# Order of statistics, keys and shared weights around the attention loop of a gated cross-attention and expert layer

## The reference

```
x = x + tanh(g_xattn) * LN'( attention( LN(x), context ) )       # 16 heads of 64, one learned null key and value
h = LN(x)
x = x + tanh(g_ffn) * ( shared_expert(h) + sum over the 8 best of 32 experts of weight * expert(h) )
expert(h) = ( silu(h Wg + bg) * (h Wu + bu) ) Wd + bd            # 256 -> 128 -> 256
weight = sigmoid(logit) / sum of the 8 sigmoids
```

## Time and profile before

| | us |
|---|---|
| median of 3 runs | 2310.6 |
| lowest, highest | 2310.09, 2318.49 |
| the profiled execution | 2310.3 |
| its span | 2308.6 |

### The profile page before, as it was taken

How to read it: one execution, slowest core, us unless ns; L and a number is a source line. 1 busy time by engine, 2 the same in 40 slices (tenths; PEclk the granted TensorE clock), 3 DMA queues, 4 the chain that set the end, 5 groups by cost and what they waited for, 6 DMA issues and landing times. The chain is left out here.

```text
span 2308.6 us, 44550 instructions
## 1 busy us (share of the span) xinstructions
PE 2080.1 (90%) x14386; PEld 1908.5 (83%) x14386; DVE 1837.3 (80%) x4287; ACT 1532.5 (66%) x4478; POOL 1299.8 (56%) x1444
## 2 busy tenths in 40 slices
PE   8999679999999999999998599999999999999992
PEld 7888578888889899888888478988888888888881
DVE  5444357888888888888888566877999999999994
ACT  5433346676767777766766235888888887888881
POOL 1000213777777777777777540001777777777776
PEclk9999889999999999999999799999999999999996
DMA  9987489987878878787887699989999999999995
GB/s 318 322 284 263 137 281 311 323 267 256 264 263 267 265 246 264 261 266 257 267 264 243 204 389 357 298 296 303 398 405 405 402 397 393 390 398 394 395 394 170
DMA packets 385092, 708.51 MB, mean 307 GB/s; under 512 B 136380, under 2 KB 248989, under 8 KB 382397
## 3 DMA queue, kind: packets, MB, share of 16 engines
q1 hardware_dynamic: 335708, 562.99, 70.1%
q0 software_dynamic: 49152, 142.67, 16.9%
HBM read 348.18 MB, written 357.30 MB: 306 GB/s over the span
## 5 line engine op out<-in xcount | busy, mean ns | idle before, releaser
L1472 POOL DMA_INDIRECT parts<-results_dram,kept_index x512 | 531.6, 1038 | 411.2 <-DMA results_dram<-y 246.0
L776 POOL DMA_INDIRECT pages_dram<-rows,kept_index x472 | 473.2, 1003 | 138.1 <-issue 120.0
L845 ACT ACTIVATE exps<-sim,minus_max 128x78 f32<-128x78 f32 x1024 | 319.1, 355 | 37.9 <-DVE minus_max L923 35.1
L1503 ACT ACTIVATE y<-yps,row_weight 128x256 f32<-128x256 f32 x636 | 246.9, 470 | 1.2 <-PE yps L134 1.2
L845 ACT ACTIVATION_READ_ACCUMULATOR exps<-sim,minus_max 128x1 f32 x1024 | 240.3, 235 | 0.0
L1494 ACT ACTIVATE w_h<-w_raw 128x768 fp32r<-128x768 f32 x159 | 137.3, 863 | 85.4 <-DMA w_raw<-in_experts 85.3
L1681 PE MATMUL xps<-ident,xin 128*128 128x128 f32 x1272 | 168.6, 276 | 28.1 <-DVE wq_l L1543 16.0
L132 PE MATMUL yps<-w_h,hid_h 128*128 128x256 f32 x636 | 179.4, 282 | 2.1 <-ACT y L1503 2.1
L133 PE MATMUL yps<-w_h,hid_l 128*128 128x256 f32 x636 | 179.8, 283 | 0.0
L134 PE MATMUL yps<-w_l,hid_h 128*128 128x256 f32 x636 | 179.2, 282 | 0.0
L1524 ACT ACTIVATE hid_h<-hidden 128x512 fp32r<-128x512 f32 x175 | 110.2, 630 | 101.4 <-DVE hidden L1634 96.9
(11 more groups left out here) (270 smaller groups left out, 7530.8 us busy)
## 6 DMA issues: line engine op xcount, KB each, us to landing
xin<-pages_dram SPq DMA_DIRECT2D x159, 576.0 KB, 9.6
results_dram<-y SPq DMA_DIRECT2D x159, 512.0 KB, 8.8
pages_dram<-blank SPq DMA_DIRECT2D x108, 576.0 KB, 3.6
w_raw<-in_experts SPq DMA_DIRECT2D x159, 385.0 KB, 9.3
pages_dram<-blank SPq DMA_DIRECT2D x12, 1728.0 KB, 7.0
keys_h_dram<-keys_h SPq DMA_DIRECT2D x32, 624.0 KB, 5.8
keys_l_dram<-keys_l SPq DMA_DIRECT2D x32, 624.0 KB, 7.6
kT_h<-keys_h_dram SPq DMA_DIRECT2D x32, 624.0 KB, 5.6
```

What stands on the lines that cost most here:

```text
L776: pool.indirect_dma_start(dram["pages"], bass.IndirectOffsetOnAxis(ap=kept_index[:, at:at + 1].bitcast(U32), axis=0), buffer(batch)[:, k / ...
L845: last = act.activation(exps[u % 2][:, h, :], scores(u)[:, h // 4, h % 4, :], ACT.Exp, bias=minus_max[u][:, h:h + 1], accum_out=row_sum[u] ...
L1472: pool.indirect_dma_start(parts[slot(batch, t)][:, k, :], None, done, bass.IndirectOffsetOnAxis(ap=kept_index[:, at:at + 1].bitcast(U32), ...
L1503: last = act.activation(y[s][:, q, :], yps[:, q, :], ACT.Copy, scale=row_weight[s][:, q:q + 1])
```

## The change

Five edits, all in the order of the lists:

- **Statistics.** VectorE works kind 0 right behind kind 2 at T3b instead of at Q3. GpSimd makes its rstd right behind that of kind 2, ahead of scatter 12. ScalarE applies kind 2 behind PV1a's high half instead of ahead of it.
- **First scores.** Units 0 and 1 wait for the low half of Q1 and no longer of Q3; they use heads of Q0 and Q1 only. Units 2 and 3 still wait for Q3.
- **Keys and null rows.** In iteration 0 SyncE waits for the scores and loads batch 1's keys ahead of the first fill and of the values. The null rows of the second value buffer are placed behind batch 1's values in iteration 0, with a semaphore of their own; those of the first stay in iteration -1.
- **Shared weights.** VectorE and ScalarE scale and split them in iteration 32 behind N2, not in iteration 33 ahead of it.
- **Last store of weights.** The semaphores of the routing weights live across the two stages; the wait for the last batch's goes from the attention stage's end to load 4 of the expert stage.

```diff
@@ attention_phase, SyncE
+            def place_nulls(i):
+                rest = v_rest[i][:, :, :, :, :].rearrange("p s f q d -> p (s f) q d")
+                for head in range(PAIRS):
+                    sp.dma_start(rest[(head + 1) * REST - 1:(head + 1) * REST, :, head // 2, head % 2 * DH:(head % 2 + 1) * DH].bitcast(F32),
+                                 null_rows[:, :, :, :].rearrange("p s f d -> p (s f) d").bitcast(F32)).then_inc(null_placed[i], 16)
...
+                if b == 0:
+                    sp.wait_ge(sim_full, UNITS)
+                    load_keys(1)
                 fill_pages(b, 0)
...
-                    for v in v_rest:
-                        rest = v[:, :, :, :, :].rearrange("p s f q d -> p (s f) q d")
-                        for head in range(PAIRS):
...
+                    place_nulls(0)
+                if b == 0:
+                    place_nulls(1)
                 fill_pages(b, 1)
-                if 0 <= b <= B - 2:
+                if 1 <= b <= B - 2:
                     sp.wait_ge(sim_full, UNITS * (b + 1))
                     load_keys(b + 1)
...
             for i in range(BUFFERS):
-                sp.wait_ge(weights_stored[i], 16 * len(range(i, B, BUFFERS)))
+                if i != (B - 1) % BUFFERS:
+                    sp.wait_ge(weights_stored[i], 16 * len(range(i, B, BUFFERS)))
@@ GpSimd
                 if 1 <= b <= B:
                     make_rstd(2, b - 1)
+                if b <= B - 3:
+                    make_rstd(0, b + 2)
                 if scatters:
                     scatter(b, range(12, 13))
...
-                if b <= B - 3:
-                    make_rstd(0, b + 2)
@@ ScalarE
-                if b == B + 1:
-                    act.wait_ge(shared_gated, 1)
...
+                    if name == "N2" and b == B:
+                        act.wait_ge(shared_gated, 1)
+                        act.activation(ahead["shared_split"][0][:, :], shared[:, :], ACT.Copy).then_inc(shared_hi, 1)
...
-                    if name == "Q3" and 1 <= b <= B:
+                    if name == "PV1a" and 1 <= b <= B:
...
                         apply(2, buffer(b - 1)[:, :, 0:D], lambda t: x1[1 - par][:, t, :], b - 1)
@@ VectorE
-                if b == B + 1:
-                    dve.wait_ge(ahead_loaded, 144)
...
+                    if name == "N2" and b == B:
+                        dve.wait_ge(ahead_loaded, 144)
...
                     if name == "T3b" and 1 <= b <= B:
                         dve.wait_ge(summed, b)
                         statistics(2, lambda t: x1[1 - par][:, t, :], b - 1)
+                    if name == "T3b" and b <= B - 3:
+                        dve.wait_ge(x_loaded, 16 * (b + 2))
+                        statistics(0, lambda t: x_in[:, t, :], b + 2)
...
-                    if name == "Q3" and b <= B - 3:
-                        dve.wait_ge(x_loaded, 16 * (b + 2))
-                        statistics(0, lambda t: x_in[:, t, :], b + 2)
@@ TensorE
-                pe.wait_ge(ring_lo, nth(EVICTED, "Q3", b - 1))
+                pe.wait_ge(ring_lo, nth(EVICTED, "Q3" if u // 2 else "Q1", b - 1))
...
-                    if b == 0:
-                        pe.wait_ge(null_placed, 32 * PAIRS)
+                    if b <= 1:
+                        pe.wait_ge(null_placed[b], 16 * PAIRS)
@@ expert_phase, SyncE
             def load_weights(n):
                 if n >= DEPTH:
                     sp.wait_ge(x_full, DC * (n - DEPTH + 1))
+                if n == DEPTH:
+                    last = (B - 1) % BUFFERS
+                    sp.wait_ge(weights_stored[last], 16 * len(range(last, B, BUFFERS)))
```

More of the change, by code:

```diff
@@ L459, in weight_views, with attention_phase @@
             w[:, 2 * DC * I:EW])
-def attention_phase(nc, ctx, dram, wq, wo, opened_by, rows, kept_index, ahead):
+def attention_phase(nc, ctx, dram, wq, wo, opened_by, rows, kept_index, ahead, weights_stored):
     def sb(name, shape, dt=F32):
@@ L554, in attention_phase @@
     x1_stored = [sem(f"x1_stored{i}") for i in range(2)]
-    weights_stored, scattered = ([sem(f"{n}{i}") for i in range(BUFFERS)] for n in ("weights_stored", "scattered"))
+    scattered = [sem(f"scattered{i}") for i in range(BUFFERS)]
     x2_stored = sem("x2_stored")
@@ L1059, in step @@
                     prepare()
-                if b == B + 1:
-                    dve.wait_ge(ahead_loaded, 144)
[L1062 to L1068, removed]
-                    dve.tensor_tensor(ahead["bias_stack"][low_rows, :], bias_rows[low_rows, :],
-                                      ahead["bias_stack"][low_rows, :].bitcast(F32), ALU.subtract)
-                    dve.tensor_tensor(shared_row_split[1][:, :], shared_row[:, :], shared_row_split[0][:, :].bitcast(F32),
-                                      ALU.subtract).then_inc(shared_row_ready, 1)
                 if here:
@@ L1081, in step @@
                     low(name, b)
+                    if name == "N2" and b == B:
+                        dve.wait_ge(ahead_loaded, 144)
+                        down = shared[:, 2 * DC * I:EW]
+                        dve.tensor_scalar(shared_row[:, :], shared_row[:, :], gate2[0:1, 1:2], None, ALU.mult)
+                        dve.tensor_scalar(down, down, gate2[:, 1:2], None, ALU.mult).then_inc(shared_gated, 1)
+                        dve.wait_ge(shared_hi, 3)
+                        dve.tensor_tensor(ahead["shared_split"][1][:, :], shared[:, :],
+                                          ahead["shared_split"][0][:, :].bitcast(F32), ALU.subtract)
+                        low_rows = slice(2 * ROUTED, 3 * ROUTED)
+                        dve.tensor_tensor(ahead["bias_stack"][low_rows, :], bias_rows[low_rows, :],
+                                          ahead["bias_stack"][low_rows, :].bitcast(F32), ALU.subtract)
+                        dve.tensor_tensor(shared_row_split[1][:, :], shared_row[:, :], shared_row_split[0][:, :].bitcast(F32),
+                                          ALU.subtract).then_inc(shared_row_ready, 1)
                     if name == "T3b" and 1 <= b <= B:
@@ L1233, in xT_ahead, with expert_phase @@
     return [[w[:, :, i * PAGE:(i + 1) * PAGE] for w in wq] for i in range(INNER // PAGE)]
-def expert_phase(nc, ctx, dram, opened_by, rows, kept_index, ahead, wq):
+def expert_phase(nc, ctx, dram, opened_by, rows, kept_index, ahead, wq, weights_stored):
     def sb(name, shape, dt=F32):
@@ L1749, in sb @@
             return across.enter_context(nc.sbuf_tensor(name, shape, dt))
+        weights_stored = [across.enter_context(nc.semaphore(f"weights_stored{i}")) for i in range(BUFFERS)]
         opened_by = sb("opened_by", [P, B * ROUTED])
```

15 lines of the change are left out of this document (6 added, 9 removed).

## The result

| | before | after |
|---|---|---|
| median, us | 2314.6 (4 runs) | 2351.4 (4 runs) |
| profiled execution, us (its span) | 2310.3 (2308.6) | 2356.1 (2354.4) |

The changed kernel takes 1.0165 times as long [1.0145, 1.0184]: 37 us more by the medians, 46 between the two profiled executions. The direction was forecast, the size wasn't: 14 us were forecast, and 2351.4 lies outside the range of 2294 to 2334.

The account below looks back on a forecast made before the run. The loop was taken as bound by first maximum, exponentials, unit 3's scores, TensorE to Q0 and VectorE's backlog. 2310.3 + 19.5 (loop) - 3 (opening) - 2.6 (end) gave 2324 us; range 2294 to 2334.

Parts of the forecast that it names:

- What sets the period: Regular iteration, 30.07 us: first maximum, two units of exponentials, unit 3's scores, TensorE to Q0, VectorE's backlog, next maximum.
- the wait for X: TensorE's transposes of normalised tokens waited 34.7 us in the loop; removing this was to gain 0.0 an iteration, bounds 0 to 1.3.
- The collision: GpSimd's earlier product z times scale holds VectorE's L937 and L938 of unit 3: +1.08 an iteration, +29.2 us.
- Rival (a): VectorE's L937 goes ahead of GpSimd's product; period and half-clock time stay: 2305 us, chance 0.24.
- (b): VectorE goes first and the half-clock stretches vanish with the wait for X: 2286 us, chance 0.10.
- (c): The opening keeps its 8.90 us as gain and VectorE goes first: 2299 us, chance 0.08.
- 8.90: TensorE's wait in us for batch 1's keys, issued behind its values; forecast to go when the keys are issued first.
- Half clock: Loop iterations with TensorE's clock at 0.50: six as before, 1.52 each, 9.1 us in place of 18.8.
- T3a's wait: TensorE's transposes T3a wait for the outputs' low half; forecast to grow by 1.08 us in a regular iteration.
- rival (d): As forecast, but half the loop's iterations hold a half-clock stretch, eight more: 2336 us, chance 0.08.
- The opening: Up to batch 4: keys 1's wait goes, keys 2's becomes some 11 us; -3 us, bounds +1 and -9.
- The end: Last iterations: weight split moves into VectorE's idle (1.6 us), SP's store wait leaves (0.98); -2.6 us, bounds 0 and -4.

Follow-up runs that it names:

- after_product_later: Changed kernel with one more GpSimd scatter ahead of the product z times scale and one fewer behind its sum; 2312.8 us, 1.0005 of before.
- before_product_earlier: Kernel before with one GpSimd scatter moved from ahead of the product z times scale to behind it; 2331.4 us, 1.0082 of before.

## Why the prediction was wrong in size

**What sets the period: right.** X no longer waits in the loop, and the scores of unit 3 start at 1005.98, 0.15 behind unit 1's last row sum. The idle moved as said, 1.18 in two pieces (0.26 and 0.92) where 1.1 was forecast ahead of unit 3's alone. That the wait for X wasn't worth its 34.7 us was shown by the pair of kernels with the product later: 0.08 of regular period an iteration.

**The collision: right by its mechanism, with luck in the margin.** GpSimd came 0.55 earlier against the first maximum, just what was asked (0.55) and less than the 0.64 to 0.77 that I had found; the scatter in front took 1.40 instead of 1.04 and ate the rest. So the head start of 0.05 was there only in the 12 iterations with a stretch behind the scores' idle. In the 15 others the product is recorded 0.01 behind L945, and L945 is held all the same: that the tie went this way no row had shown. L945 takes 1.79 to 1.88 in every iteration, the period is 31.24 (forecast 31.15), and 26 x 31.24 + 30.13 for the last one is 842.4: +30.5 against +29.2. In the kernel before, the product moved by one scatter gave the same 31.18. Rival (a) fell: L937 won in no iteration of the changed kernel, and with it fell (b) and (c), of which (c) also had the whole 8.90 kept as a gain at batch 4. By the rule of the Trainium skill ("SBUF — State Buffer", "Who interferes with whom") whichever of the two issues first holds the port; the three positions of the product agree (L937 of unit 3 at 1.79 with the product 0.05 ahead, 0.69 with L938 at 1.37 when it is 0.54 behind, 0.69 and 0.27 when it comes after both). For the tie of 0.01 the recorded starts can't tell who issued first.

**Half clock: the step that failed.** I took six stretches "as before, since the idle time that remains is as long", at 1.52 each: 9.1. There are 26, 12 behind the scores' idle and 14 behind T3a's wait. What is over the regular periods is 872.7 - 842.4 = 30.3, against 18.8 before: +11.5 instead of -9.7, and this 21.2 is two thirds of the 31.9 us by which the two profiled executions differ from the forecast's +13.9. The price was right where I had it: an iteration with a stretch behind the scores' idle alone takes 32.78, 1.54 more. Its count was wrong, 12 for six, some 9 us. What I left out is a second kind, 14 at about 0.9 each (32.15), some 12 us, 21 to 23 us behind the first maximum and just behind T3a's wait. The prediction had that wait growing by 1.08 and gave it no stretch. Its upper bound, one iteration in three, was a guess, too low; rival (d) had the direction, and its 2336 the same fault. Whether each place of idle alone does it was then measured: T3a's 1.34 with X's 1.27 makes 6, the scores' 1.19 alone 9 (after_product_later), and only with T3a's 1.34 and the scores' 1.19 together are there 24 and 26. In the loops of these kernels all stretches but one begin just behind one of these waits. Why this pair is hit so much more often than the pair in before_product_earlier isn't settled. The length of the wait alone doesn't decide it: in the kernel before X waits 1.3 in all 27 iterations, and six of the seven stretches come in every fourth iteration, 122.88 us apart. The Trainium skill ("TensorE: Matmul & The Clock Gate", "HAM oscillation — how this bites in real kernels") has gaps let the clock fall, in its example waits for a DMA of some 3 to 5 us; the trace agrees that it falls behind gaps, in the kernels before and after with waits of 0.92 to 1.44 us just in front, but the sum of TensorE's three longest waits in the loop, 62.5 us before and 76.9 after, doesn't give 7 and 26.

**The opening: wrong mechanism.** Forecast -3, measured +4.1 (+3.0 alone). The steps around it:

```profile
282.91 0.34 SPq L611 DMA_DIRECT2D kT_h<-keys_h_dram  x1
...
284.24 6.21 SPq L621 DMA_DIRECT2D v_main<-values_dram  x2
...
300.66 4.95 SPq L665 DMA_DIRECT2D v_rest<-null_rows  x8
...
335.38 1.00 SPq L611 DMA_DIRECT2D kT_l<-keys_l_dram  x1
...
345.23 0.47 PE L132 MATMUL sim<-kT_h,qT_h 128*128 128x156 f32 x1 [15.73 <-issue]
...
389.31 1.64 POOL L784 DMA_INDIRECT pages_dram<-rows,kept_index  x1 [8.60 <-DMA pages_dram<-blank]
```

The 8.90 did go, as forecast. Keys 2 were to be issued about 331.5 and come in at 342; they were issued at 335.38 and the scores waited 15.73 instead of 11. SP stands still until 282.9 for unit 3's scores, v_main behind the keys takes 6.21 instead of 3.42, and with the second null rows the fill behind stands at 305.7 and not 302.3. But by the runs above the mis-sized SP queue isn't what set batch 4: it follows GpSimd's first scatter, which waits for the fills. The kernel before shows GpSimd waiting 9.42 for them at 386.81, and I read TensorE's waits there, not GpSimd's.

**The end: right steps, wrong bound.** The profile of after:

```profile
1324.10 0.76 DVE L952 BATCH_NORM_STATS2 stats<-ring 128x6 f32<-128x256 f32 x2 [1.44 <-PE ring L134]
...
1337.47 0.69 DVE L1058 TENSOR_TENSOR x2T_l<-ring,x2T_h 128x512 fp32r<-128x512 f32 x1 [2.30 <-ACT x2T_h L865]
...
1346.94 0.17 DVE L1050 TENSOR_SCALAR kept_index<-top_key 128x16 int32<-128x16 f32 x1
...
1352.24 0.20 POOL L1464 MEMSET ident<- 128x128 f32 x1 [7.51 <-POOLq L606]
```

Measured from the low half of N2 that precedes the split (1271.72 in the kernel before, 1318.12 here: 46.40 on), VectorE's statistics come at the same time (1277.70, 1324.10), so the split is covered; the last low half of N2 comes 1.48 sooner (forecast 1.6), and so does the routing's last row. But the expert stage starts only 0.59 sooner. In the kernel before:

```profile
1302.01 0.17 DVE L1042 TENSOR_SCALAR kept_index<-top_key 128x16 int32<-128x16 f32 x1
...
1306.43 0.20 POOL L1451 MEMSET ident<- 128x128 f32 x1 [7.51 <-POOLq L606]
```

In both kernels, and in every other kernel of the study, it starts 7.51 behind the end of GpSimd's last scatter, while VectorE's idle at this place is 4.35 in one and 5.23 in the other. SyncE's waits ended at 1303.7 in the kernel before, 2.7 ahead of the stage. GpSimd's queue bounded this end; the store's landing (0.98) was hidden, so taking SP's wait away was worth nothing. -2.6 should have been -0.6.

**The sum.** With the half clock as measured it would have been +13.9 + 21.2 = +35, and with the opening and the end +44; the profiled executions differ by 45.8.

## What to carry to other kernels

Ask of a wait of the busiest engine whether another wait stands behind it: this one was 34.7 us long and worth 0.08 of regular period an iteration, until VectorE's backlog was cut; then the same edit was worth 0.66. When an edit makes a queue earlier, list what its instructions will meet: GpSimd 0.55 us earlier cost 1.17 an iteration, and one scatter moved, or 0.65 us of VectorE's backlog moved, turned the same change from 1.0165 to 1.0005 and 0.9870 of before. At the opening and at a stage's end read the waits of every queue for the one that ends last, GpSimd's too, before any other is given a price.

## What was not expected of the hardware

- The number of half-clock stretches isn't a sum over idle time: 7 with 1.27 us ahead of X, 6 with that and 1.34 ahead of T3a, 9 with 1.19 ahead of the scores, 26 with 1.19 and 1.34.
- The race for the port has the same winner in all 27 iterations of the changed kernel (in the kernel before it turns in six of 27), though in 15 of them the two starts are 0.01 us apart; a move that puts the product 0.36 or more behind turns it in all.
- A group's mean hides it: L937 has a mean of 959 ns over its 108 instructions in the loop before and 979 in that after, although unit 3's went from 0.69 to 1.86. Unit 0's, which had met GpSimd's x plus bias (1.53), no longer does (0.69).
- The kernel before took 2803 and 2868 us on two chips, with stops of 7 us on VectorE and ScalarE. One of them bears the number of a chip that gave 2312.5 earlier.
- GpSimd's last scatter of a stage and the first instruction of the next are 7.51 us apart in every kernel of the study.
